# Bidirectional decay gates in a four-stage network: the backward scan made to run over the forward scan, tiles handled in pairs with one reciprocal, and the thirteen attention-stage tiles done in the expert stage

## The reference, cut to what matters

```python
def gate(x, f, w, u, cond):
    tf = sigmoid(sum(cond))
    decay = exp(-exp(w)) * (0.5 + 0.5 * tf)
    ek = exp(min(f, 30)); euk = exp(min(u + f, 30))
    nf, df = scan(a * decay + ek * f), scan(b * decay + ek)
    nb, db = the same two, from the last token to the first
    num = nf + nb - ek * f + euk * f
    den = df + db - ek + euk
    return sigmoid(x) * num / max(den, 1e-8) * (0.8 + 0.2 * tf)
x = x + mamba2(gate(x, f, ...))
x = x + moe(gate(x, f, ...))
x = x + attention(gate(x, f, ...))
x = x + ffn(gate(x, f, ...))
```

## Time and profile before

| | |
|---|---|
| median of 3 runs | 2923.15 us (2921.53 to 2926.87) |
| profiled execution | 2925.15 us |
| its span | 2923.4 us |
| mean granted TensorE clock | 0.912 of full speed |
| TensorE matmuls busy | 2298.2 us (79%) |
| TensorE weight loads busy | 1689.5 us (58%) |
| Vector busy | 2052.2 us (70%) |
| ScalarE busy | 909.9 us (31%) |
| GpSimd busy | 719.4 us (25%) |

### The profile page before, as it was taken

The page is one execution under the profiler, slowest core; times in us unless marked ns, Lnnn a source line. Parts: engine busy times, 40 slices in busy tenths (PEclk is TensorE's granted clock), DMA queues, the critical chain, the costliest instruction groups (busy, mean ns, idle before and its releaser), DMA issues.

```text
span 2923.4 us, 33508 instructions
## 1 busy us (share of the span) xinstructions
PE 2298.2 (79%) x10207; PEld 1689.5 (58%) x10208; DVE 2052.2 (70%) x2931; ACT 909.9 (31%) x1891; POOL 719.4 (25%) x566
## 2 busy tenths in 40 slices
PE   0568868768777389977856888798979988899998
PEld 0234334334333167765745667677767776688887
DVE  8889889889888746656654556666666667566665
ACT  2123223223223232233322334333433443422222
POOL 2234234235244223423331102211121212000000
PEclk9988989889889689988977889899989999999999
DMA  4001001001002423233141100001000100100001
GB/s 174 15 22 40 18 14 43 15 22 36 15 22 75 149 94 104 71 137 133 61 143 59 29 18 29 22 7 36 22 7 25 47 22 22 51 22 22 23 20 58
DMA packets 51464, 141.93 MB, mean 49 GB/s; under 512 B 5760, under 2 KB 5760, under 8 KB 47056
## 3 DMA queue, kind: packets, MB, share of 16 engines
q1 hardware_dynamic: 32192, 91.72, 9.1%
...
## 4 chain that ended last, share of the span: by engine, by line
issue 49%; PE 20%; POOL 12%; POOLq 9%; DVE 5%; ACT 2%; DMA 1%; ACTq 0%; DVEq 0%; SPq 0%
PE bank L328 6%; PE bank L329 6%; PE bank L330 6%; POOLq L453 3%; POOLq L466 3%; POOLq L463 3%; POOL g_v L454 2%; POOL g_e L462 2%; POOL g_eu L464 2%; POOL g_v L470 2%; PE bank L1862 1%; POOL aw_lo L414 1%; POOLq L681 1%; POOL ug L682 1%; DVE rinv L1567 1%
## 5 line engine op out<-in xcount | busy, mean ns | idle before, releaser
L1762 PE MATMUL bank<-um,w_in 128*128 128x512 f32 x576 | 284.2, 647 | 72.2 <-DVE state L1260 27.7
L1762 PEld LDWEIGHTS bank<-um,w_in 128*128 128x128 f32 x576 | 114.8, 208 | 219.0 <-issue 128.4
L973 ACT ACTIVATE probs<-bank,nmx 128x128 f32<-128x128 f32 (+3 forms) x256 | 131.5, 526 | 175.9 <-DVE nmx L1570 175.9
L328 PE MATMUL bank<-u_hi,aw_hi 128*128 (+1 forms) x384 | 162.6, 423 | 9.4 <-issue 9.4
L328 PE MATMUL bank<-pt_hi,v_hi 128*128 128x512 f32 (+3 forms) x256 | 91.0, 355 | 90.4 <-DVE pt_lo L1585 87.6
L461 POOL TENSOR_TENSOR g_ek<-g_ek,g_r 128x511 f32<-128x511 f32 x47 | 66.4, 1413 | 378.1 <-DVE g_ek L440 378.1
L1585 DVE TENSOR_TENSOR pt_lo<-bank,pt_hi 128x512 fp32r<-128x512 f32 (+1 forms) x192 | 109.1, 596 | 70.8 <-ACT pt_hi L980 70.8
L448 DVE RECIPROCAL g_ek<-g_eu 128x512 f32<-128x512 f32 x47 | 157.6, 3353 | 1.6
L329 PE MATMUL bank<-u_lo,aw_hi 128*128 (+1 forms) x384 | 154.0, 401 | 0.0
L330 PE MATMUL bank<-u_hi,aw_lo 128*128 (+1 forms) x384 | 153.8, 401 | 0.0
L980 ACT ACTIVATE pt_hi<-bank 128x512 fp32r<-128x512 f32 (+1 forms) x192 | 93.8, 525 | 157.5 <-PE bank L1862 157.5
...
## 6 DMA issues: line engine op xcount, KB each, us to landing
...
```

The costliest lines, as they stand in the source:

```text
L328: nc.tensor.matmul(out, hi_w, hi_x, start=start, stop=False)
L973: A(probs[:, h % 2, PR_AT[qb]:PR_AT[qb] + w], S_[bk][:, c0:c0 + w], ACT.Exp, bias=nmx[:, h % 2, qb:qb + 1], scale=SCALE, accum_out=rsum[:, ...
L1762: mm = M(dst[:], w_in[:, k, c0:c0 + P], um[:, k, :], start=(k == 0), stop=(k == KC - 1))
```

## The change

**The sums.** Before, the backward scan ran over the inputs and was added to the forward scan. Now the forward scan runs in place, is turned into the two-sided sum by a second scan in place, from the last token to the first, and the two additions that joined the scans go. For this the clamp of `ek` also multiplies by `inflow` = 1 - decay², and one small instruction multiplies the last column of both forward scans by `edge` = 1 / inflow. The decay is held below 1 by `DECAY_MAX`.

**Pairs.** A job is now two tiles: one 512 KB load and store in place of two of 256 KB, and one reciprocal. GpSimd multiplies the two denominators, Vector inverts the product, and GpSimd multiplies the inverse by either denominator to get the other's inverse. `g_v` has four slots. Vector does 17 counted steps for a pair and GpSimd 9.

**Places.** The 30 pairs lie one in setup, 4 in each Mamba batch (16), and 13 in the expert stage, one for each triple; attention has none. GpSimd's list in the expert stage is the products of both tiles, first gather, additions of tile 0, second gather, additions of tile 1, third gather, a drain, the product of the denominators, the result of the pair.

**The expert stage's order.** TensorE transposes the inner activations before `up_glu` (before, behind it); ScalarE's `by_hi` and Vector's `by_lo` stand first in their lists (before, behind the expert switch and `glu`); the output buffer `m_o` has two slots in place of three. The last pair is finished before the output gathers, and SP waits for all gate stores before it loads attention weights.

**Scores.** The masks are added behind all four strips, with three matmuls in place of four.

**Buffers.** `txm` lies over `lm`, the expert stage's `tanh` inputs over `xdt`, `rms_inv` over `e2`.

```diff
+V_CLAMPED, V_FORWARD, V_EDGE, V_SUMS, V_DENS, V_PAIR = (2, 9), (4, 11), (5, 12), (7, 14), (15, 16), 17
+P_PRODUCTS, P_ADDED, P_DENS, P_READY, P_PAIR = (1, 2), (4, 6), 7, (8, 9), 9
...
+        def gate_clamp(eng, k, s, t):
+            _, _, ek, eu = g_tile(s, t)
+            eng.wait_ge(g_exp, k * 4 + (2 * t + 2))
+            nc.vector.tensor_scalar(ek, ek, EXP30, inflow[:, bass.ds(k * 2 + (G_VEC + t), 1)], ALU.min, ALU.mult).then_inc(g_vec, 1)
+            nc.vector.tensor_scalar(eu, eu, EXP30, None, ALU.min).then_inc(g_vec, 1)
+        def gate_scans(eng, k, s, t):
+            _, e, ek, _ = g_tile(s, t)
+            n = k * 2 + (G_VEC + t)
+            d = decay[:, bass.ds(n, 1)].to_broadcast([P, T])
+            scan = nc.vector.tensor_tensor_scan
+            eng.wait_ge(g_pool, k * P_PAIR + P_PRODUCTS[t])
+            for x in (e, ek):
+                scan(x, d, x, 0.0, ALU.mult, ALU.add).then_inc(g_vec, 1)
+            eng.wait_ge(g_vec, k * V_PAIR + V_FORWARD[t])
+            end = g_s[:, t, :, T - 1]
+            nc.vector.tensor_scalar(end, end, edge[:, bass.ds(n, 1)], None, ALU.mult).then_inc(g_vec, 1)
+            eng.wait_ge(g_vec, k * V_PAIR + V_EDGE[t])
+            for x in (e, ek):
+                scan(x[:, ::-1], d, x[:, ::-1], 0.0, ALU.mult, ALU.add).then_inc(g_vec, 1)
+        def gate_dens(eng, k, s):
+            for t in range(2):
+                _, e, _, eu = g_tile(s, t)
+                eng.wait_ge(g_pool, k * P_PAIR + P_ADDED[t])
+                nc.vector.tensor_scalar(e, eu, 1e-8, oscale[:, bass.ds(k * 2 + (G_VEC + t), 1)], ALU.max, ALU.mult).then_inc(g_vec, 1)
+        def gate_inverse(eng, k, s):
+            r = g_tile(s, 1)[2]
+            eng.wait_ge(g_pool, k * P_PAIR + P_DENS)
+            nc.vector.reciprocal(r, r).then_inc(g_vec, 1)
...
+        def gate_add(eng, k, s, t):
+            v, e, ek, eu = g_tile(s, t)
+            eng.wait_ge(g_vec, k * V_PAIR + V_SUMS[t])
+            nc.gpsimd.tensor_tensor(eu, eu, ek, ALU.add).then_inc(g_pool, 1)
+            nc.gpsimd.tensor_tensor(v, v, e, ALU.add).then_inc(g_pool, 1)
+        def gate_result(eng, k, s):
+            (v0, d0, _, _), (v1, d1, r, _) = g_tile(s, 0), g_tile(s, 1)
+            mult = nc.gpsimd.tensor_tensor
+            eng.wait_ge(g_vec, k * V_PAIR + V_PAIR)
+            mult(d1, r, d1, ALU.mult)
+            mult(d0, r, d0, ALU.mult)
             eng.drain()
...
+            mult(v0, v0, d1, ALU.mult).then_inc(g_pool, 1)
+            mult(v1, v1, d0, ALU.mult).then_inc(g_pool, 1)
...
             sp.wait_ge(dn_done, FIRST + NBLK)
-            for i in range(3):
-                sp.wait_ge(y_stored[i], FIRST_DMA + 16 * (NBLK // 3))
+            for i in range(2):
+                sp.wait_ge(y_stored[i], FIRST_DMA + 16 * ((NBLK + 1 - i) // 2))
+            for i in range(2):
+                sp.wait_ge(g_out[i], FIRST_DMA + 16 * (N_PAIRS // 2))
...
+            def pair_gate(k, s, gathers=((), (), ())):
+                for t in range(2):
+                    gate_products(pool, k, s, t)
+                for t in range(2):
+                    for j, q in gathers[t]:
+                        gather(j, q)
+                    gate_add(pool, k, s, t)
+                for j, q in gathers[2]:
                     gather(j, q)
...
+                (_, d0, _, _), (_, d1, r, _) = g_tile(s, 0), g_tile(s, 1)
+                pool.drain()
+                pool.wait_ge(g_vec, k * V_PAIR + V_DENS[1])
+                nc.gpsimd.tensor_tensor(r, d0, d1, ALU.mult).then_inc(g_pool, 1)
+                gate_result(pool, k, s)
...
-            slot_gate(*moe_tile(NBLK // 6, 0)[:2], between=first_outputs)
+            pair_gate(*moe_pair(NBLK // 6, 0))
+            first_outputs()
...
-                if q == 0:
-                    gate(n, slot, use)
+                k, s = moe_pair(pair, h)
+                act.wait_ge(ty_done, j + 1)
+                A(by_hi[:].rearrange("p k t -> p (k t)"), TP[:], ACT.Copy).then_inc(by_hi_ready, 1)
                 if not (last and q == 2):
                     with act.If(flags[q] != 0):
                         e = act.value_load(tab[0:1, 1, j + 1:j + 2] if last else tab[0:1, 1, bass.ds(j + 1, 1)], min_val=1, max_val=E - 1)
                         act.wait_ge(dn_done, FIRST + j)
                         split_hi(e, e % 2)
                     up_tanh(j + 1, (q + 1) % 3)
-                act.wait_ge(ty_done, j + 1)
-                A(by_hi[:].rearrange("p k t -> p (k t)"), TP[:], ACT.Copy).then_inc(by_hi_ready, 1)
                 if not (last and q >= 1):
                     u_hi_copy(j + 2)
+                if q == 0:
+                    gate((k, s), 1)
+                if q == 2 and not last:
+                    gate((k + 1, 1 - s), 0)
+                o = (3 * h + q) % 2
                 act.wait_ge(dn_done, FIRST + j + 1)
-                act.wait_ge(y_stored[q], FIRST_DMA + 16 * it)
-                A(m_o[:, q, :], DN[:], ACT.Copy, scale=0.5).then_inc(out_copied, 1)
-                if q == 1:
-                    g_store(act, n - 1, 1 - slot)
-                if q == 2 and not last:
-                    g_load(act, n + 1, 1 - slot, moe_tile(pair, h + 1)[2])
+                act.wait_ge(y_stored[o], pair * 48 + (FIRST_DMA + 16 * ((3 * h + q) // 2)))
+                A(m_o[:, o, :], DN[:], ACT.Copy, scale=0.5).then_inc(out_copied, 1)
+                if q == 0:
+                    g_store(act, k - 1, 1 - s)
+                if q == 1 and not last:
+                    g_load(act, k + 1, 1 - s)
...
+                    if q == 1:
+                        clamp(mamba_pair(b, 0), 0)
+                    elif q == 3:
+                        scans(mamba_pair(b, 0), 0)
+                        clamp(mamba_pair(b, 0), 1)
+                    elif q == 5:
+                        scans(mamba_pair(b, 0), 1)
+                    elif q == 8:
+                        dens(mamba_pair(b, 0))
...
-                    gate(mamba_tile(b, 2 if tb else 1), tb - 1 if tb else 2)
+                    if tb == 0:
+                        inverse(mamba_pair(b, 0))
+                        clamp(mamba_pair(b, 1), 0)
+                    elif tb == 1:
+                        scans(mamba_pair(b, 1), 0)
+                        clamp(mamba_pair(b, 1), 1)
+                    elif tb == 2:
+                        scans(mamba_pair(b, 1), 1)
+                    else:
+                        dens(mamba_pair(b, 1))
...
-                gate(mamba_tile(b, 3), 0)
+                inverse(mamba_pair(b, 1))
...
+                    now = mamba_pair(b, 2 + j // 4)
+                    if j % 4 == 0:
+                        if j:
+                            inverse(mamba_pair(b, 2))
+                        clamp(now, 0)
+                    elif j % 4 == 1:
+                        scans(now, 0)
+                        clamp(now, 1)
+                    elif j % 4 == 2:
+                        scans(now, 1)
                     else:
-                        gate(mamba_tile(b, 3 + j // 2), 2)
-                        gate(mamba_tile(b, 4 + j // 2), 0)
-                gate(mamba_tile(b, 7), 1)
+                        dens(now)
+                inverse(mamba_pair(b, 3))
...
             def block_dve(pair, h, q, flags, last):
                 j = pair * 6 + (3 * h + q)
+                dve.wait_ge(by_hi_ready, j + 1)
+                V.tensor_tensor(flat(by_lo[:]), TP[:], flat(by_hi[:]).bitcast(F32), ALU.subtract).then_inc(y_split, 1)
+                k, s = moe_pair(pair, h)
+                if q == 2:
+                    dens((k, s))
                 if not (last and q == 2):
                     with dve.If(flags[q] != 0):
                         e = dve.value_load(tab[0:1, 1, j + 1:j + 2] if last else tab[0:1, 1, bass.ds(j + 1, 1)], min_val=1, max_val=E - 1)
                         split_lo(e, e % 2)
                     glu(j + 1, (q + 1) % 3)
-                dve.wait_ge(by_hi_ready, j + 1)
-                V.tensor_tensor(flat(by_lo[:]), TP[:], flat(by_hi[:]).bitcast(F32), ALU.subtract).then_inc(y_split, 1)
-                if not (last and q == 2):
                     inner(j + 1, (q + 1) % 3)
                 if not (last and q >= 1):
                     select(j + 2, (q + 2) % 3)
                     u_lo_split(j + 2)
-                gate(moe_tile(pair, h), q)
+                if q == 0:
+                    scans((k, s), 0)
+                    clamp((k, s), 1)
+                elif q == 1:
+                    scans((k, s), 1)
+                else:
+                    inverse((k, s))
+                    if not last:
+                        clamp((k + 1, 1 - s), 0)
...
                 if not last:
                     q_lo_split(i + 1, 1)
                 pt_lo_split(i, 3, (0, 1))
-                with_gate(lambda: gate_scans(dve, n, a_ek[:], a_e[:], a_r1[:], a_r2[:]))
...
             def block_pe(it, q, last):
                 j = it * 3 + q
```

(13 more changed lines are left out.)

321 lines of the change are left out of this document (129 added, 192 removed).

## The result

The changed kernel takes 2928.59 us and the kernel before 2922.30 us, each the median of 17 runs side by side: a ratio of 1.0021, with an interval of 1.0014 to 1.0029. That is 6.3 us slower, where 2906, some 17 us faster, was forecast: the time lies inside the stated range, and the direction is wrong. The profiled execution has a span of 2928.0 us, against 2923.4.

What follows compares the result with a forecast made beforehand. Vector was 89% busy in Mamba; TensorE bounded the expert stage and stalled on `pt_lo` in attention. Attention -97, masks -10, expert stage +76, Mamba +16, setup -2 gave -17: 2906 us median, range 2855 to 2950.

Steps and rivals of the forecast that it cites:

- the eleven rings: Expert stage: a closed loop of waits through TensorE, Vector and GpSimd per triple adds 112 us; +68 with cheaper expert switches.
- inside a ring the split falls mostly into Vector's waits ... 2 each remain: Expert stage: six later expert switches fall from 9.3 us each to 2, -44 us in all.
- The other half of that step: Expert switches: `by_lo` placed early removes TensorE's wait, part of the -44 us.
- The ring's length: Expert stage: a regular triple takes 40.6 us against 30.4 before, the first gather's landing delaying TensorE's transposes.
- The rival of stretched products: Expert stage: GpSimd's products each take 0.35 us more beside Vector; ring 44.5 us, time 2949 us; chance 0.22.
- Mamba: Four Mamba batches: net +4 us a batch, +16 in all, bounds -29 to +40.
- The tail is TensorE's: End of each Mamba batch: TensorE's output products end after Vector's scans, so Vector work removed there gains nothing.
- The second rival: Mamba returns its Vector work: -29 us in place of +16, time 2861 us; chance 0.16.
- Attention: Attention stage: removing gate tiles ends `pt_lo` stalls (-76.6 us) and raises the clock, -97; masks -10; -107 in all.
- The masks: Attention's causal masks: fewer weight loads save 10 us, between 0 and 34.5.
- the clock term: Attention: without stalls TensorE no longer runs at half clock behind them, 21 us less.
- The transition: Block 36 to first attention product: `by_lo` behind scans +5 us, later result, store and load +3; +8 in all.

Runs made afterwards that it cites:

- the last run: Changed kernel with gathers one place forward, the expert-stage clamp swap, and attention weights loaded ahead of the wait for gate stores: 2839.15 us, ratio 0.9711.
- the 34 us triple: Three expert blocks in the changed kernel with gathers one place forward and tile 1's clamp ahead of tile 0's scans there: 34.3 us; run 2846.57 us, ratio 0.9734.

## Why the prediction failed, point by point

**The direction was lost in one term.** The forecast of -17 against a measured +4.6 in the profiled executions is off by 21.6, and the eleven rings alone by 34. The step that failed is "inside a ring the split falls mostly into Vector's waits ... 2 each remain". Vector's wait for GpSimd in the ring is 3.67 us, read above, and the split is 9.24 behind a wait of 1.54. Where it lies between the clamp and the scans, reciprocal's end to the next scans takes 15.2 us (1303.1 to 1318.3), in a regular ring 8.7 (1179.9 to 1188.6). Where it follows tile 1's clamp, there is no such wait to fall into: it holds up GpSimd's last product, index copy and first gather by 5.2 us, and in two of these three rings the gather then lands late beside the next weights. The six rings cost 38.9 us over regular ones, not 12. I had the two numbers when I wrote it (a split of over 9 us, GpSimd's result and products of 8.2, of which Vector's own block work takes about 5) and did not subtract them. The run with the split cut returned 27 us, which is the sign of the result by itself. Of the 34 us this step is 27; the other terms of the forecast that were off took the sum the other way.

**The other half of that step** was that `by_lo` first in the lists removes TensorE's stall. In the kernel before, where no ring covers it, the new order gave 17 us, of waits that had come to 54: most of them passed to `bu_lo`. An instruction moved out from behind a long one leaves the long one in the list.

**The ring's length** was forecast at 40.6 us and is 41.4 in the mean of the five regular rings: right, link by link, and 9 us over eleven rings. But the reading that the first gather was *the* link to cut was too simple. With that gather ahead of the products the triple only went to 40.3 in the mean of three; the loop also closes through Vector's scans and `by_lo`. It opens where GpSimd issues gathers in time that it would spend waiting for Vector (76 us), or where the second clamp leaves the scans' shadow (46 us in the rings, 30 with Mamba's loss).

**Slower side.** The rival of stretched products is seen, but only at the switches: in the ring of 1283.6 to 1331.7 three of GpSimd's products took 3.31, 2.67 and 3.13 us, and in three others a product, a copy and a gather were stretched, all beside Vector's weight split. In a regular ring the products took 1.26 to 1.47, not the 1.64 that the rival needed on every one. The clamp of the earlier trace rows on which it leaned reads one tensor, the split two.

**Mamba** measured +19.0 for +16, and that is luck: two errors cancel. By parts of a batch, after less before, for the four batches in turn (us):

| part | change | forecast each |
|---|---|---|
| batch's start to the first input product | -1.5, -4.8, -5.8, -5.4 | 0 |
| convolutions | -1.8, -3.7, -2.6, -3.0 | -3.7 |
| four token blocks | +8.7, +6.7, +8.5, +8.5 | +6.5 |
| eight pairs | +4.1, +4.8, +3.8, +2.4 | +1.3 |

The token blocks and the pairs together cost 16 us more than forecast. The joints between batches gave 16 us back, where the prediction had "The tail is TensorE's" and "What leaves Vector there gains nothing". That step failed. TensorE's first input product of the third batch, before and after, one fence each:

```profile
531.66 8.69 PE L1762 MATMUL bank<-um,w_in 128*128 128x512 f32 x15 [6.67 <-DVE dt L1183]
```

```profile
535.36 10.15 PE L1797 MATMUL bank<-um,w_in 128*128 128x512 f32 x19 [0.91 <-DVE dt L1204]
```

The prediction compared the end of Vector's scans (511.75) with the end of the output products (521.5) and left out what Vector still had to do: a second reciprocal, from 520.07, and additions to 528.2 (2.9 us of idle time behind them have no releaser in the profile). So Vector, not TensorE, was late at every joint, and the change took most of that away. Behind the fourth it shows in the stretch to block 0, -12.7 where nothing was forecast: the output products end 15.9 us later and the router starts only 4.6 later, since its wait for Vector fell from 14.80 to 3.45 us. The moved reciprocal gives 4.2 of these 11.3 us back and, at the joints, only 0.4 to 0.6; the tile whose scans left the tail is the likely rest, which no run shows alone. The second rival had these tails right, and like the forecast it missed the cost ahead of them.

**Attention** measured -114.5 for -107: TensorE waits 74.0 us less and is busy 40.5 less (836.9 to 796.4). The waits for `pt_lo` ahead of the output products fell by 78.1 (76.6 forecast); others grew by 4. The masks gave 10.5 (10): against the run with the old ones TensorE is busy 13.4 us less and waits 3 more. The other 27 us of busy time are the clock term (21 forecast): the granted clock rose from 0.92 to 0.95 with nearly the same matmuls. By the Trainium skill, TensorE: Matmul & The Clock Gate, Part 1, the throttled state is the default and activity releases it; the trace agrees in both directions, with 1.00 in an iteration without stalls and 0.50 behind each of the twelve gathers waited for from block 3 on.

**The transition** measured +14.0 for +8. The last block, behind scans of the last pair, takes 8.8 of it: 28.3 us from the last transposes of `ug` to its output copy, 19.5 before (5 forecast). The other 5.2 (3 forecast) fit the chain result, store, wait, load, of which the last run took 5.7 out in a kernel with another expert stage.

What stays open: what the weights' load costs when it does not start beside a gather, since no run moved it; what took the joints' 16 us away, Vector's scans or its reciprocals; and which of Vector's neighbours stretches it in the 34 us triple.
